# A decoder megakernel: its first layer reordered and written as a straight line

## The chip, the cores and the metric

One core of a Trainium2 chip runs the whole program in one launch. The metric is the device time of that core in microseconds, the median of several executions. The core's engines work from queues of their own, in order, and wait for each other through semaphores: TensorE (PE; its weight loads are PEld), VectorE (DVE), ScalarE (ACT), GpSimd (POOL) and SyncE (SP), which here only issues transfers.

## What is computed

Two decoder layers on x of 64 sequences x 128 tokens x 128 channels, all in float32, each sublayer followed by `x = layernorm(x + f(x))`: a linear attention with a cumulative sum, a cross attention of 16 heads, a mixture of experts, a selective scan, a second cross attention and a quantised feed-forward. The change touches only the first sublayer:

```python
def _L0_attn_ref(x, w_qkv, w_swiglu, w_out):
    qkv = jnp.einsum('btd,ed->bte', rms_norm(x), w_qkv)
    q, k, v = jnp.split(qkv, 3, axis=-1)
    q, k = rms_norm(q), rms_norm(k)
    w = jnp.exp(k)
    kv = jnp.cumsum(w * v, axis=1)
    w = jnp.cumsum(w, axis=1)
    y = jax.nn.sigmoid(q) * (kv / (w + 1e-06))
    u, g = jnp.split(jnp.einsum('bte,fe->btf', y, w_swiglu), 2, axis=-1)
    return x + jnp.einsum('btd,ed->bte', u * jax.nn.silu(g), w_out)

x = _layernorm(x + _L0_attn_ref(x, ...), axis=-1)
```

## The kernel before

`build` lays out memory, runs `setup`, and then six phases one after the other (a: `phase_aft`, b: first cross attention, m: experts, s: scan, c: second cross attention, q: feed-forward). x stays on the chip as [128 tokens, 64 sequences, 128]. Between phases stand full barriers: `open_signals` has SyncE raise every semaphore of the phase by one, `close_signals` has GpSimd clear them, and `finish_statistics` turns the batch-norm statistics that a phase left into mean and 1/deviation.

`setup` (L96, L102): SyncE asks for the four weights of phase a, ScalarE for the 45 others, one after the other; GpSimd sets constants. `phase_aft` first waits for the weights of a and s (ident is among the latter), then opens its block.

In `phase_aft` the 64 sequences go in 16 groups of GB = 4, so that a tile is 128 x 512. SyncE loads x group by group, each after the last has landed (L273), and then writes 33 fills of 1040 KB to DRAM for phase m (L278). Every other engine runs `in_group_steps`: three steps written out, a loop over g (1 to 13), three written out. A step works on several groups at once, by letters: a is group g+2, b g+1, c g, d g-1. The order within a step is fixed for each engine:

- TensorE: q, k and v of g+1 (`project`, L448, one signal after all twelve products), turning y of g (L468), turning x of g+2 (L439), g and u of g (`up`, L475, L478, one signal), sums of w and of w*v of g+1 (L458, L461, one signal), down product of g (L484).
- ScalarE: squares of x of g+2 (L316), squares of q and k of g+1 (L328, L331), copy of yT (L351), exp and tanh of g+1 (L339, L344), copy of xnT (L323), tanh of g (L356).
- GpSimd: 1/rms of x (L285, L288) and of q and k in one (L294, L298).
- VectorE: `mean_y` of g (add 1e-6 to den L391, reciprocal L394, gate L397, y L401), normalise x of g+2 (L380), `add_up` of g-1 (2x + o into `total` L415, statistics L167, copies into x and `core.stats` L169, L171), `weigh` of g+1 (w*v, L386), `hidden` of g (L407, L410).

All eight PSUM banks are in use, one tile each: turn, q, k, v, wsum, kvsum, u, g; the turned y goes into wsum's bank and the down product into u's. A signal's value in the loop is computed from g by register instructions.

Of the kernel before, what the change touches and what calls it, by code (L numbers as in the profile page):

```python
# [7 lines left out]
F32 = mybir.dt.float32  # L8
# [17 lines left out]
FILLS = 33  # L26
NO_ROW = 1e6
# [59 lines left out]
def setup(core):  # L87

    nc = core.nc
    with nc.Block() as block:  # L90
# [72 lines left out]
def leave(dve, nc, core, g, steps, total, stats):  # L163

    dve.wait_ge(steps.sem, steps.at(g, 1))
    for j in range(GB):
        last = nc.vector.bn_stats(stats[:, j, :], total[:, j, :])  # L167
    last.then_inc(steps.sem, 1)
    nc.vector.tensor_copy(core.x[:, ds(g * GB, GB), :], total[:, :, :])  # L169
    dve.wait_ge(steps.sem, steps.at(g, 2))  # L170
    nc.vector.tensor_copy(core.stats[:, ds(g * GB, GB), :], stats[:, :, :]).then_inc(steps.sem, 1)  # L171


def leave_one(dve, nc, core, i, steps, total, stats):

    dve.wait_ge(steps.sem, steps.at(i, 1))
    nc.vector.bn_stats(stats, total).then_inc(steps.sem, 1)
    nc.vector.tensor_copy(core.x[:, i, :], total)
    dve.wait_ge(steps.sem, steps.at(i, 2))
    nc.vector.tensor_copy(core.stats[:, i, :], stats).then_inc(steps.sem, 1)  # L180


def in_group_steps(eng, step):


    step(-2, "a")
    step(-1, "ab")
    step(0, "abc")
    with eng.Fori(1, NG - 2) as g:
        step(g, "abcd")  # L190
    step(NG - 2, "bcd")
    step(NG - 1, "cd")
    step(NG, "d")

def phase_aft(core):
    nc = core.nc  # L200
    x = core.x
    with ExitStack() as ctx:
# [14 lines left out]
        qk_ms = sb("a_qk_ms", [128, 2, GB])  # L217
        xn = sb("a_xn", [128, GB, 128])
        xnT = sb("a_xnT", [128, GT])
# [8 lines left out]
        total = sb("a_total", [128, GB, 128])  # L228
        stats = sb("a_stats", [128, GB, 6])
# [9 lines left out]
        o_ps = u_ps.rearrange("p (b d) -> p b d", b=GB)  # L239

        x_in = sig("a_x_in", 16)
# [6 lines left out]
        qkv_ready = sig("a_qkv_ready")  # L248
        qk_squared = sig("a_qk_squared")
        qk_eps = sig("a_qk_eps")  # L250
        qk_rms = sig("a_qk_rms")
# [30 lines left out]
        def _(pool):  # L282
# [19 lines left out]
            def step(g, stages):  # L302
                if "a" in stages:
                    x_rms_of(g + 2)
                if "b" in stages:
                    qk_rms_of(g + 1)
# [2859 lines left out]
```

## Time and profile before

| | us |
|---|---|
| median of 3 runs | 3586.96 (3586.45 to 3598.22) |
| profiled execution | 3601.83 |
| its span, first to last instruction | 3600.0 |
| of it: until the first square of x | 30.8 |
| first phase's last VectorE instruction ends | 258.9 |
| first instruction of the next phase on ScalarE | 266.6 |

Over the whole span TensorE is busy 77%, VectorE 70%, GpSimd 53%, ScalarE 47%; the granted TensorE clock was 0.892 of full on average. The first phase fills slices 1 to 3 of the page's forty (90 us each):

```profile
PE   4767887879878827777777777857999999998455
PEclk9988999978999958989889889998999999998555
DMA  5701000001144433333333333320000000000000
```

A digit is a share in tenths. TensorE is busy at 4, 7 and 6 tenths in the three slices, and DMA at 5, 7 and 0.

### The profile page before, as it was taken

What the parts mean: (1) busy time and instruction counts of PE and PEld (TensorE: products, weight loads), DVE (VectorE), ACT (ScalarE), POOL (GpSimd) and SP (SyncE); (2) the same over time, 40 slices, a digit from 0 to 9 for tenths busy, and PEclk for the clock granted to TensorE, in tenths of its full rate; (3) what the DMA queues carried; (4) which work ended last, traced back from release to release, by engine and by line L of the source; (5) the groups of instructions that cost most, each with busy time, mean ns of one, the idle gap of its engine ahead of it and who ended that gap; (6) DMA issues with size and microseconds to landing.
All of it is one profiled execution on the core that took longest, in us unless ns stands there. A gap on an engine that the chain in (4) does not pass through costs nothing. (4 is left out here: it accounts for less than half of the span.)

```text
span 3600.0 us, 53795 instructions
## 1 busy us (share of the span) xinstructions
PE 2787.7 (77%) x16569; PEld 1638.9 (46%) x16584; DVE 2503.4 (70%) x4015; ACT 1708.7 (47%) x3190; POOL 1897.4 (53%) x1698
## 2 busy tenths in 40 slices
PE   4767887879878827777777777857999999998455
PEld 3435555555645512323333333324666666666222
DVE  3768888845533335988988989994666666664787
ACT  3546666633222216555555555543444444443565
POOL 1216777745545546767767767762333333332444
PEclk9988999978999958989889889998999999998555
DMA  5701000001144433333333333320000000000000
GB/s 184 328 2 24 18 17 17 10 24 35 35 125 131 127 96 148 126 127 141 110 127 139 115 125 137 130 82 6 3 5 5 4 4 5 5 3 1 9 17 21
DMA packets 130113, 249.03 MB, mean 69 GB/s; under 512 B 41057, under 2 KB 97910, under 8 KB 109314
## 3 DMA queue, kind: packets, MB, share of 16 engines
q1 hardware_dynamic: 114480, 223.49, 18.1%
q0 software_dynamic: 9088, 16.94, 1.4%
q10 hardware_dynamic: 6354, 6.27, 0.6%
q8 instruction: 93, 1.52, 0.2%
q14 instruction: 98, 0.80, 0.1%
HBM read 189.34 MB, written 59.13 MB: 69 GB/s over the span
## 5 line engine op out<-in xcount | busy, mean ns | idle before, releaser
L1753 POOL TENSOR_TENSOR s_drive<-s_du,s_b_sb 128x1024 f32<-128x1024 f32 x256 | 602.1, 2355 | 288.0 <-DVE s_state_ps L1979 287.8
L1979 DVE TENSOR_TENSOR_SCAN s_state_ps<-s_decay_ps,s_drive 128x512 f32<-128x512 f32 x512 | 600.2, 1218 | 124.6 <-ACT s_decay_ps L1886 62.6
L2092 PE MATMUL s_y_ps<-s_read,w_ident 128*128 128x512 f32 x1024 | 540.6, 661 | 187.9 <-DVE s_read L1993 187.6
L1886 ACT ACTIVATE s_decay_ps<-s_delta,neg_rate 128x508 f32<-128x508 f32 x512 | 348.3, 686 | 388.9 <-DVE s_state_ps L1979 388.7
L2092 PEld LDWEIGHTS s_y_ps<-s_read,w_ident 128*128 128x128 f32 x1024 | 198.6, 207 | 512.3 <-DVE s_read L1993 298.7
L1993 DVE TENSOR_TENSOR s_read<-s_state_ps,s_c_sb 128x1024 f32<-128x1024 f32 x256 | 313.3, 1224 | 12.7 <-DVE s_state_ps L1979 1.4
L2315 ACT ACTIVATE c_pT<-c_turn_ps 77x512 f32<-77x512 f32 x256 | 148.7, 585 | 248.7 <-PE c_turn_ps L2516 248.6
L2249 POOL TENSOR_TENSOR x<-c_xs,w_c_bo 128x128 f32<-128x128 f32 x64 | 31.1, 486 | 427.4 <-DVE c_xs L2355 427.4
L1372 POOL DMA_INDIRECT m_y_scratch<-e_y,e_index x156 | 152.6, 978 | 135.6 <-DVE e_index L1406 56.5
L697 ACT ACTIVATE b_pT<-b_turn_ps 77x512 f32<-77x512 f32 x256 | 145.0, 590 | 117.8 <-PE b_turn_ps L822 117.8
L631 POOL TENSOR_TENSOR b_p<-b_p,b_top 128x1232 f32<-128x1232 f32 x64 | 143.9, 2248 | 93.9 <-DVE b_top L754 93.9
L2372 DVE TENSOR_TENSOR c_v<-c_f_ps,w_c_bv 77x512 f32<-77x512 f32 x128 | 87.9, 687 | 148.5 <-PE c_f_ps L2486 148.5
L2271 POOL TENSOR_TENSOR c_p<-c_p,c_norm 128x1232 f32<-128x1232 f32 x64 | 143.8, 2247 | 70.6 <-DVE c_norm L2395 70.6
L996 POOL DMA_INDIRECT m_rows_scratch<-m_xs,m_index x128 | 126.9, 991 | 100.3 <-DVE m_xs L1124 59.8
L2323 ACT ACTIVATE c_oT<-c_f_ps 128x512 f32<-128x512 f32 x128 | 76.4, 597 | 207.1 <-PE c_f_ps L2534 207.1
L2546 PE MATMUL c_turn_ps<-w_c_wo,c_oT 128*128 128x128 f32 x1024 | 136.2, 289 | 45.7 <-ACT c_pT L2315 44.9
L822 PE MATMUL b_turn_ps<-w_ident,b_p 128*77 128x128 f32 x1024 | 160.4, 291 | 14.3 <-POOL b_p L637 14.2
L2546 PEld LDWEIGHTS c_turn_ps<-w_c_wo,c_oT 128*128 128x128 f32 x1024 | 125.5, 200 | 73.5 <-issue 72.6
L637 POOL TENSOR_TENSOR b_p<-b_p,b_norm 128x1232 f32<-128x1232 f32 x64 | 143.9, 2248 | 22.0 <-DVE b_norm L760 21.9
L2516 PEld LDWEIGHTS c_turn_ps<-w_ident,c_p 128*77 128x77 f32 x1024 | 123.5, 148 | 69.3 <-issue 47.6
L2516 PE MATMUL c_turn_ps<-w_ident,c_p 128*77 128x128 f32 x1024 | 153.9, 278 | 1.0 <-ACT c_pT L2315 1.0
L2377 DVE TENSOR_REDUCE c_top<-c_s_ps 128x16 f32<-128x1232 f32 x64 | 92.3, 1441 | 81.7 <-PE c_s_ps L2500 81.7
(366 smaller groups left out, 6535.8 us busy)
## 6 DMA issues: line engine op xcount, KB each, us to landing
s_b_sb<-s_bc_scratch SPq DMA_DIRECT2D x64, 1024.0 KB, 4.6
s_c_sb<-s_bc_scratch SPq DMA_DIRECT2D x64, 1024.0 KB, 4.7
m_rows_scratch<-fill SPq DMA_DIRECT2D x33, 1040.0 KB, 26.2
e_w<-in_m_we_dram SPq DMA_DIRECT2D x39, 384.0 KB
e_xg<-m_rows_scratch SPq DMA_DIRECT2D x39, 260.0 KB
k_y<-m_y_scratch SPq DMA_DIRECT2D x32, 256.0 KB, 3.8
x<-in_x_dram SPq DMA_DIRECT2D x16, 256.0 KB, 2.8
out_dram<-q_result SPq DMA_DIRECT2D x16, 256.0 KB, 2.3
```

The lines of the kernel that those rows point to most:

```text
L631: nc.gpsimd.tensor_tensor(p[:, s, :, :], p[:, s, :, :], top[:, s, :].unsqueeze(2).broadcast_to([128, heads, S2]), ALU.subtract).then_inc(l ...
L697: nc.scalar.activation(pT[:, j, :, :], turn_ps[0:S2, j % 2, :].rearrange("p (r t) -> p r t", t=128), ACT.Copy).then_inc(pT_ready.sem, 1)
L822: last = nc.tensor.transpose(turn_ps[0:S2, j % 2, r * 128:(r + 1) * 128], p[:, s, per * r + j, :], core.ident[:, :])
L1372: nc.gpsimd.indirect_dma_start(y_dram[:, :], bass.IndirectOffsetOnAxis(index[:, t % y_slots, j:j + 1], 0), y[:, t % y_slots, j, :], None, ...
L1753: nc.gpsimd.tensor_tensor(drive[:, n % 2, :, :], du[:, s, :, :], b_sb[:, n, :].unsqueeze(1).broadcast_to([128, halves, GT]), ALU.mult).the ...
L1886: nc.scalar.activation(decay[:, m, :, 1:], delta[:, s, m, :].rearrange("p (b t) -> p b t", t=T)[:, :, 1:], ACT.Exp, scale=core.neg_rate[:, ...
L1979: nc.vector.tensor_tensor_scan(state[:, h, :], decay[:, h, :, :].rearrange("p b t -> p (b t)"), drive[:, n % 2, h, :], 0.0, ALU.mult, ALU. ...
L1993: nc.vector.tensor_tensor(read[:, n % deep, :, :], state[:, :, :], c_sb[:, n // per_chunk % 2, n % per_chunk, :].unsqueeze(1).broadcast_to ...
L2092: last = nc.tensor.matmul(y_ps[:, m, :], core.ident[:, :], read[:, n % deep, m, :], start=False, stop=(n == states - 1))
L2315: nc.scalar.activation(pT[:, per * r:per * (r + 1), :], turn_ps[0:S2, r % 2, :].rearrange("p (j t) -> p j t", t=128), ACT.Copy).then_inc(p ...
L2516: last = nc.tensor.transpose(turn_ps[0:S2, r % 2, j * 128:(j + 1) * 128], p[:, i % 2, per * r + j, :], core.ident[:, :])
L2546: last = nc.tensor.matmul(y_ps, oT[:, b, :], core.w["c_wo"][:, b, :], start=(b == 0), stop=(b == blocks - 1))
```

## The change

- `setup`: ScalarE asks for the first three groups of x and no weight; SyncE asks for the weights of phase a, ident now first among them. The other weights follow on SyncE in the phase, after the loads of the other 13 groups of x and before the fills.
- No wait ahead of the phase's block; TensorE alone waits for its weights.
- No loops: `over_periods` writes out 21 steps from g = -4 to 16 for all engines. Stages are further apart: squares and normalisation of x at g+4, turning x at g+3, projections at g+2, sums and y at g+1, up at g, down and the addition at g-1.
- q, k and v have signals of their own, k first; so have the squares of q and k, the two sums, and g and u. xnT has two buffers.
- Normalising x moves from VectorE (four instructions) to GpSimd (one on 128x512). GpSimd's 1/rms of q and k is split in two. Adding 1e-6 to den moves from VectorE to ScalarE (Identity with a bias).
- The turned y uses the turn bank; the down product uses v's bank, so that v of g+2 waits for the addition of g-1.
- The addition writes x in place, and the statistics go straight to `core.stats`; `total`, `stats` and both copies go.
- ident stays in memory to the end.

```diff
 def setup(core):
         @block.scalar
         def _(act):
-            for phase in "sbmcq":
-                for name in WEIGHTS[phase]:
-                    act.dma_start(core.w[name][:], core.ins[name]).then_inc(core.landed[phase].sem, 16)
+            for g in range(EARLY):
+                act.dma_start(core.x[:, g * GB:(g + 1) * GB, :],
+                              core.ins["x"][g * GB:(g + 1) * GB, :, :].rearrange("b t d -> t b d")
+                              ).then_inc(core.x_early[g].sem, 16)
...
-        o_ps = u_ps.rearrange("p (b d) -> p b d", b=GB)
+        o_ps = v_ps
...
+        def over_periods(step):
+            for g in range(-4, NG + 1):
+                step(g)
-        open_signals(nc, signals, [core.landed["a"], core.landed["s"]])
+        open_signals(nc, signals, [])
...
         def _(sp):
-            with sp.Fori(0, NG) as g:
-                sp.wait_ge(x_in.sem, x_in.at(g, 0))
+            for g in range(EARLY, NG):
+                if g > EARLY:
+                    sp.wait_ge(x_in.sem, x_in.at(g - EARLY, 0))
...
+            for phase in "bmscq":
+                for name in WEIGHTS[phase]:
+                    sp.dma_start(core.w[name][:], core.ins[name]).then_inc(core.landed[phase].sem, 16)
             for n in range(FILLS):
...
         def _(pool):
+            def normalise(g):
+                pool.wait_ge(x_rms.sem, x_rms.at(g, 1))
+                if g >= 1:
+                    pool.wait_ge(x_turned.sem, x_turned.at(g - 1, 1))
+                nc.gpsimd.tensor_tensor(xn[:, :, :], x[:, g * GB:(g + 1) * GB, :],
+                                        x_ms[:, :].unsqueeze(2).broadcast_to([128, GB, 128]),
+                                        ALU.mult).then_inc(x_normed.sem, 1)
+            def step(g):
+                if on(g + 4):
+                    x_rms_of(g + 4)
+                    normalise(g + 4)
+                if on(g + 2):
+                    k_rms_of(g + 2)
+                    q_rms_of(g + 2)
...
         def _(act):
+            def raise_den(g):
+                act.wait_ge(wsum_ready.sem, wsum_ready.at(g, 1))
+                if g >= 1:
+                    act.wait_ge(y_steps.sem, y_steps.at(g - 1, 2))
...
+                nc.scalar.activation(den[:, :], wsum_ps[:, :], ACT.Identity,
+                                     bias=den_eps[:, 0:1]).then_inc(den_ready.sem, 1)
+            def step(g):
+                if on(g):
+                    copy_yT(g)
+                if on(g + 1):
+                    raise_den(g + 1)
+                if on(g + 4):
+                    square_x(g + 4)
+                if on(g + 3):
+                    copy_xnT(g + 3)
+                if on(g + 2):
+                    square_k(g + 2)
+                    square_q(g + 2)
+                    exp_k(g + 2)
+                if on(g):
                     tanh_g(g)
+                if on(g + 2):
+                    tanh_q(g + 2)
...
         def _(dve):
             def weigh(g):
                 dve.wait_ge(w_ready.sem, w_ready.at(g, 1))
+                dve.wait_ge(v_ready.sem, v_ready.at(g, 1))
+                if g >= 1:
+                    dve.wait_ge(kvsum_ready.sem, kvsum_ready.at(g - 1, 1))
...
             def add_up(g):
+                here = x[:, g * GB:(g + 1) * GB, :]
                 dve.wait_ge(o_ready.sem, o_ready.at(g, 1))
+                nc.vector.scalar_tensor_tensor(here, here, 2.0, o_ps[:, :, :], ALU.mult,
+                                               ALU.add).then_inc(added.sem, 1)
+                dve.wait_ge(added.sem, added.at(g, 1))
+                for j in range(GB):
+                    nc.vector.bn_stats(core.stats[:, g * GB + j, :], x[:, g * GB + j, :])
+            def step(g):
+                if on(g + 1):
+                    weigh(g + 1)
+                if on(g - 1):
+                    hidden(g - 1)
+                if on(g + 1):
+                    mean_y(g + 1)
+                if on(g - 1):
+                    add_up(g - 1)
...
         def _(pe):
+            def project_v(g):
+                if g >= 1:
+                    pe.wait_ge(kv_ready.sem, kv_ready.at(g - 1, 1))
+                if g >= 3:
+                    pe.wait_ge(added.sem, added.at(g - 3, 1))
+                project(g, v_ps, 2, v_ready)
+            def step(g):
+                if on(g):
                     turn_y(g)
+                if on(g + 1):
+                    sum_w(g + 1)
+                if on(g + 3):
+                    turn_x(g + 3)
+                if on(g + 1):
+                    sum_kv(g + 1)
+                if on(g + 2):
+                    project_k(g + 2)
+                    project_q(g + 2)
+                if on(g - 1):
+                    down(g - 1)
+                if on(g):
                     up(g)
+                if on(g + 2):
+                    project_v(g + 2)
+            pe.wait_ge(core.landed["a"].sem, core.landed["a"].value)
+            over_periods(step)
```

## Rows read from the trace of the kernel before

**Rows 1.** Eight periods: us; busy us PE, PEld, DVE, ACT, POOL; clock; DMA share; GB/s.

```profile
102.35:204.73 102.38, 75.33 (x386) 48.07 (x385) 80.42 (x144) 56.69 (x280) 24.92 (x33) 0.97 0.57 237
```

**Rows 2.** One period on VectorE; timeline: start, us, engine, line, operation [idle before].

```profile
102.35 3.35 DVE L394 RECIPROCAL a_den<-a_den 128x512 f32<-128x512 f32 x1
...
107.16 0.86 DVE L380 TENSOR_SCALAR a_xn<-x,a_x_ms 128x128 f32 x4
107.94 0.68 DVE L415 SCALAR_TENSOR_TENSOR a_total<-x,a_u_ps 128x512 f32<-128x512 f32 x1
...
109.44 0.41 DVE L169 COPY x<-a_total 128x512 f32 x1
...
113.10 0.69 DVE L407 SCALAR_TENSOR_TENSOR a_th_g<-a_th_g,a_g_ps 128x512 f32<-128x512 f32 x1 [1.31 <-ACT a_th_g L356]
...
114.43 0.68 DVE L391 TENSOR_SCALAR a_den<-a_wsum_ps 128x512 f32<-128x512 f32 x1
```

**Rows 3.** TensorE in the same period.

```profile
101.77 1.16 PE L484 MATMUL a_u_ps<-w_a_woutT,a_h 128*128 128x128 f32 x8 [1.29 <-DVE a_h L410]
...
104.55 1.06 PE L448 MATMUL a_v_ps<-w_a_wqkvT,a_xnT 128*128 128x128 f32 x8
107.30 0.66 PE L468 MATMUL a_wsum_ps<-w_ident,a_y 128*128 128x128 f32 x4 [1.69 <-DVE a_y L401]
...
111.32 1.10 PE L458 MATMUL a_wsum_ps<-a_w_kv,w_upper 128*128 128x512 f32 x2 [0.54 <-ACT a_w_kv L339]
```

**Rows 4.** ScalarE and GpSimd in the same period.

```profile
101.78 1.01 POOL L288 TENSOR_TENSOR a_x_ms<-a_x_ms,minus_half 128x4 f32<-128x4 f32 x1
...
105.65 0.28 ACT L328 ACTIVATE a_square<-a_q_ps 128x128 f32<-128x128 f32 x1 [4.22 <-PE a_v_ps L448]
...
108.17 1.72 POOL L298 TENSOR_TENSOR a_qk_ms<-a_qk_ms,minus_half 128x8 f32<-128x8 f32 x1
...
109.93 1.14 ACT L339 ACTIVATE a_w_kv<-a_k_ps,a_qk_ms 128x128 f32<-128x128 f32 x4 [1.26 <-POOL a_qk_ms L298]
...
112.42 0.66 ACT L356 ACTIVATE a_th_g<-a_g_ps 128x512 f32<-128x512 f32 x1
```

**Rows 5.** The opening: last weight request, table load, first square.

```profile
22.33 0.46 ACTq L102 DMA_DIRECT2D w_q_wd<-in_q_wd_dram  x1
24.88 1.28 ACT L316 ACT_TABLE_LOAD   x1 [24.88 <-PEq L54]
...
30.79 0.31 ACT L316 ACTIVATE a_square<-x 128x128 f32<-128x128 f32 x1 [4.63 <-DMA x<-in_x_dram]
```

**Rows 6.** TensorE's first projection of q.

```profile
36.20 2.07 PE L448 MATMUL a_q_ps<-w_a_wqkvT,a_xnT 128*128 128x128 f32 x8 [0.69 <-ACT a_xnT L323]
```

**Rows 7.** VectorE: first and last reciprocal, last instruction of the phase.

```profile
51.66 3.35 DVE L394 RECIPROCAL a_den<-a_den 128x512 f32<-128x512 f32 x1
...
243.06 3.35 DVE L394 RECIPROCAL a_den<-a_den 128x512 f32<-128x512 f32 x1
...
258.73 0.17 DVE L171 COPY stats<-a_stats 128x24 f32<-128x24 f32 x1
```

**Rows 8.** GpSimd by line, whole span: 128x512 multiplication and addition; busy, mean ns.

```profile
L1512 POOL TENSOR_TENSOR k_y<-k_y 128x512 f32<-128x512 f32 x16 | 22.2, 1391 | 24.0 <-DMA k_y<-m_y_scratch 23.9
...
L2711 POOL TENSOR_TENSOR q_xs<-q_xs,rstd 128x512 f32<-128x512 f32 x16 | 16.9, 1058 | 3.5 <-POOL q_xs L2707 3.2
```

**Rows 9.** ScalarE in the next phase: Exp (L691), then Identity (L672).

```profile
281.60 1.23 ACT L691 ACTIVATE b_p<-b_p 128x1232 f32<-128x1232 f32 x1 [0.95 <-POOL b_p L631]
282.74 0.48 ACT L672 ACTIVATE b_xs<-x,b_shift,rstd 128x128 f32<-128x128 f32 x1
```

**Rows 10.** SyncE's requests: start, us until the last one is issued, count.

```profile
25.18 49.87 SPq L273 DMA_DIRECT2D x<-in_x_dram  x16
75.26 62.87 SPq L278 DMA_DIRECT2D m_rows_scratch<-fill  x33
```

**Rows 11.** From issue to landing, the 33 fills (L278).

```profile
DMA to landing us min/median/max: 4.9/26.2/30.2
```

More of the change, by code:

```diff
@@ L160, in _ @@
                                            ALU.add, ALU.mult).then_inc(folded, 1)
[L163 to L193, printed above, removed]
 def phase_aft(core):
@@ L302, in step @@
[L302 to L306, printed above, removed]
-            in_group_steps(pool, step)
+            def normalise(g):
[5 more added lines that the diff above has]
+                                        ALU.mult).then_inc(x_normed.sem, 1)
@@ L335, in exp_tanh, with square_k @@
[L335 to L337 removed]
+                if g >= 2:
+                    act.wait_ge(v_ready.sem, v_ready.at(g - 2, 1))
+                nc.scalar.activation(xnT[:, g % 2, :], turn_ps[:, :], ACT.Copy).then_inc(xnT_ready.sem, 1)
+            def square_k(g):
+                act.wait_ge(k_ready.sem, k_ready.at(g, 1))
+                for j in range(GB):
+                    last = nc.scalar.activation(square[:, 1, j, :], k_ps[:, j, :], ACT.Square,
+                                                scale=D ** -0.5, accum_out=k_ms[:, j:j + 1])
+                last.then_inc(k_squared.sem, 1)
@@ L440, in turn_x @@
                 last.then_inc(x_turned.sem, 1)
-            def project(g):
-                pe.wait_ge(xnT_ready.sem, xnT_ready.at(g, 1))
-                pe.wait_ge(th_q_ready.sem, th_q_ready.at(g, 0))
-                pe.wait_ge(kv_ready.sem, kv_ready.at(g, 0))
-                for which, bank in enumerate((q_ps, k_ps, v_ps)):
-                    for j in range(GB):
-                        last = nc.tensor.matmul(bank[:, j, :], xnT[:, j * 128:(j + 1) * 128],
-                                                core.w["a_wqkvT"][:, which * 128:(which + 1) * 128],
-                                                start=True, stop=True)
-                last.then_inc(qkv_ready.sem, 1)
@@ L453, in sum_up, with project, project_k @@
-            def sum_up(g):
+            def project(g, bank, which, done):
+                for j in range(GB):
+                    last = nc.tensor.matmul(bank[:, j, :], xnT[:, g % 2, j * 128:(j + 1) * 128],
+                                            core.w["a_wqkvT"][:, which * 128:(which + 1) * 128],
+                                            start=True, stop=True)
+                last.then_inc(done.sem, 1)
+            def project_k(g):
+                pe.wait_ge(xnT_ready.sem, xnT_ready.at(g, 1))
+                if g >= 1:
+                    pe.wait_ge(w_ready.sem, w_ready.at(g - 1, 1))
+                project(g, k_ps, 1, k_ready)
```

240 lines of the change are left out of this document (117 added, 123 removed).

## The prediction

> **What bounds the kernel now.** I read the engines' busy time by stretch first, then one period of the first phase on each engine, then its opening and its end. The change touches only that phase: it holds 259 of 3600 us, so what can be won or lost lies there. In its steady part sixteen groups of four sequences pass at one every 102.38 / 8 = 12.80 us, with VectorE busy 80.42 / 8 = 10.05 us of them, ScalarE 7.1, GpSimd 3.1 [rows 1]. No engine is full. The period is a ring of waits, and the starts show it: the last product of v ends at 104.55 + 1.06 = 105.61, and the squares of q, queued on ScalarE, start at 105.65 [rows 3, 4]. GpSimd's power on 8 columns runs 108.17 to 109.89, Exp starts at 109.93, tanh of g ends at 113.08 [rows 4], VectorE goes on with th_g at 113.10 after 1.31 us of idling [rows 2], h follows, and then TensorE runs down, q, k and v in one row, as at 101.77 to 105.61 [rows 3], because all three projections stand behind the down product and ScalarE waits for v before it squares q. That is, from start to start, 2.52 (squares and GpSimd's addition) + 1.76 (power) + 3.17 (exp to tanh of g) + 1.47 (th_g and h) + 3.88 (down to v) = 12.8 us. The other thing the rows show is the opening: ScalarE asks for the last weight at 22.33, the phase's block opens at 24.88, and the first square starts at 30.79 when x has landed [rows 5]. Thirty microseconds hold no arithmetic.
>
> **The ring after the change.** It falls apart: k has its own signal, squares need q and k alone, q and k stand ahead of down, and a group's stages are spread over six periods. I looked for the rings that are left, with time zero at the end of v for group g+2.
>
> Ring A goes through VectorE and both ends of TensorE's step, since v reuses the bank of the down product: v waits for add_up(g-1), which VectorE does after the reciprocal. From zero: turning y 0.66, sum of w 1.10 [rows 3], overlapping a little, so 1.6; the new ScalarE copy with bias, costed like tanh of g with the same 128x512 from PSUM, 0.66 [rows 4], so den is there at 2.3. From the reciprocal's start to the addition's start the rows show 107.94 - 102.35 = 5.59, of which the normalisation between them (107.94 - 107.16 = 0.78) goes away: 4.81, so the addition starts at 7.1 and ends 0.68 later [rows 2], and v takes 1.06 [rows 3]. With four hand-overs of 0.04 (105.61 to 105.65) this is 9.0 us. weigh, th_g and h fit before 2.3: three instructions of 0.69. The statistics, now written straight to their place, lie beside v.
>
> Ring B goes through ScalarE and GpSimd: the squares of x (four, half of q and k's eight, 1.1 to 1.3), GpSimd's addition and power (0.27 + 1.01, rows at 101.78) [rows 4], the normalisation moved there, addition and power for k (1.3), then exp, tanh of g, tanh of q and the copy of yT (the same four kinds as 109.93 to 113.08, 3.15) and the new copy (0.5 to 0.66). The normalisation has no row in this phase. The nearest is a 128x512 multiplication with a factor per row, 1.06 us; another on 128x512 took 1.39 [rows 8]. By the first the ring is 8.7, by the second 9.0 us. I take 1.06, the same shape and operation, so it just doesn't bind.
>
> The engines alone: VectorE loses the normalisation 0.86, the addition to den 0.68, both copies 0.41 and 0.17 [rows 2, 7], so 10.05 - 2.12 = 7.9 and some gaps, 8.3. ScalarE gains 0.66: 7.8. GpSimd goes to about 5.0, since one power on 8 columns (1.72) becomes two on 4 (1.01 each) plus the normalisation; nobody but ring B waits for it. TensorE does the same work: 3.84 for down, q, k, v, four products of 1.10, two turns of 0.66 [rows 3], 9.6 if nothing overlapped, about 8.4 as neighbours do overlap (the four took 0.96 each). So the period is **9.0**, with ends 8.4 (engines alone) and 9.6 (TensorE without overlap).
>
> **Opening.** ScalarE now asks for three pieces of x, SyncE for five weights. At 0.46 each [rows 5] the latter end at 3.05. From there I copy the old distance 22.79 to 24.88, 2.09 us, and the table load of 1.28 [rows 5]. Nine more signals are raised one by one; that costs between nothing and 2.09 x 9 / 23 = 0.8, I take 0.4. x, asked for in the first microsecond, took 5.6 us from 25.18 to 30.79 [rows 5, 10] and so is there by 6.4. The first square starts at 6.9: 23.9 us gained. From the square to the first reciprocal the old kernel takes 51.66 - 30.79 = 20.9 [rows 5, 7]. The new order puts turning x of group 1 ahead of k of group 0, so this is squares 1.3, power 1.3, normalisation 1.1, all three again for group 1 (3.6), turn 1.1, k and q at the low clock 1.8 each (2.07 with the tail [rows 6]), squares and exp 1.1 each, sum of w 2.0, copy 0.7: 16.9, with hand-overs 17.3. The first reciprocal starts at 24.2.
>
> **The waits added** are mostly splits of old ones. v's wait for add_up holds the step's last product and, behind it, the turning of the next y; that is ring A. The turning of y waits for the next copy of xnT, done a period earlier. The requests for 44 weights move from ScalarE to SyncE, behind 13 loads of x (one per 49.87 / 15 = 3.3 us) and ahead of the fills [rows 10]: 5.4 + 13 x 3.3 + 44 x 0.46 puts the first fill at about 69 instead of 75, and their last request at 132. They land some 26 us later [rows 11], at 158, before this phase ends; were it to end before 150, the next phase's loads would queue behind them. The x of group 3 is asked for at 5.4 and used at 24, so loads stay hidden. Identity on ScalarE could have called for another table; in the next phase it follows Exp directly, 281.60 + 1.23 to 282.74 [rows 9], so it costs nothing. Constant waits instead of computed ones I cost at nothing: in the old period they lie beside other engines' work.
>
> **End and sum.** From the last reciprocal to the phase's last instruction: 258.90 - 243.06 = 15.8 [rows 7]. After: hidden(14) and down(14) now stand ahead of the last up product (+2), tanh of g no longer waits for u and the copies are gone (-2). I take 16.0, from 14.9 to 16.9. Intervals between reciprocals: the first 9.6 at the low clock, fourteen of 9.0. Last instruction: 24.2 + 9.6 + 126.0 + 16.0 = 175.8 instead of 258.9, 83.1 less; nine more semaphores to clear, 0.4, and rounding leave **82**. The profiled execution took 3601.83 (span 3600.0); it becomes 3520. The median of the runs is 15 us lower, 3586.96, so the forecast is **3505**. The rest of the kernel is unchanged.
>
> **What speaks against it in the notes.** In the old period a copy of 128x512 on VectorE (109.44 to 109.85, 0.41 us) ran inside GpSimd's power (108.17 to 109.89) without being held up [rows 2, 4]. The Trainium skill (SBUF — State Buffer, "SBUF: two separate sides") says that these two engines share a port pair as an exclusive lock, when VectorE's operation has two SBUF inputs or a two-port mode. By that rule the copy should have stood until 109.89; on 8 columns the trace doesn't agree. It doesn't show a GpSimd operation on 512 columns beside the gate, the one VectorE instruction of this phase with two large SBUF inputs.
>
> **Rivals.** (1) GpSimd's normalisation and the gate block each other, or ring B turns out longer than its rows. Ring A then grows by up to one normalisation, 1.06 [rows 8]: period 10.1, 16 us more, **3521**. For it: by ring A the gate comes 5.8 us after v, just where the normalisation ends. Against: the copy above. Chance 0.17. The Trainium skill's port rule, named above, would give this outcome.
> (2) Only part of the ring dissolves, the change doesn't do what it says: the period stays near 12 because some wait still ties two steps. Then opening and ramp give 27.5 and the periods 12: 27.5 + 15 x 0.8 = 39.5 less, **3547**. Chance 0.09, of it 0.02 for a ring that keeps its whole length and an opening that gains less.
> (3) The period falls to the engines' own 8.4: 9 us less, **3496**. Chance 0.10.
> (4) Slower: TensorE's clock. It had 0.97 of full over the eight periods [rows 1] and was low at the start, where q took 2.07 instead of 1.06 [rows 6, 3]. If the new order left it at the low level, its 8.4 us become 8.4 x 1.95 = 16.4 and it is the bound: 15 x 3.6 - 27.5 = 26 more, **3613**. It decides against the change from a period of 12.8 + 27.5 / 15 = 14.6. Against it: TensorE would be busier than now, idle only half a microsecond before v. Chance 0.03.
> (5) Slower: the loops are now straight code, fetched during the fills, when DMA is full. If four fetches stood on the ring for 26.2 us each [rows 11], that is 105 us: **3610**; more than three decide. Chance 0.02.
> The forecast itself has 0.59.
>
> **Range and chances.** The five ways and the forecast's own ends (period 8.7 to 9.6, opening and end 3 us, and the spread of 12 us that the three runs before show) give 3490 to 3535. A measurement here tells 0.5% from no change, so faster means below 3569: the forecast, (1), (3) and most of (2), 0.93. Same 0.02, slower 0.05.
>
> **What would show it.** The first square at 7, the first reciprocal at 24, reciprocals 9.0 apart, v waiting for the addition and the addition 4.8 after the reciprocal's start, TensorE's clock above 0.9 in the phase, the phase's last VectorE instruction at 176, and the next phase as long as before. Wrong would be: gate or reciprocal longer than 0.69 and 3.35, Exp waiting on GpSimd for over 1.5 us, idle time put down to nothing on several engines at once while fills run, or a time lost after 185 us.

## The result, and the profile after

The kernel after takes 3487.81 us in the median (3484.19 to 3497.28), the kernel before 3591.65 (3586.45 to 3598.22) in the executions taken for the comparison: a ratio of 0.9716 (0.9699 to 0.9733). The profiled execution took 3497.28 us where the old one took 3601.83, so 104.5 us of its span went, and 82 were forecast. The ends of five phases can be read off one instruction that each of them ends with, the square root in `finish_statistics`. Start of that instruction in the kernel before, and then in the kernel after:

```profile
L134 ACT ACTIVATE a_root<-rstd x1: 256/256/256, 262.8 to 262.8; 128x64 f32<-128x64 f32 x1
L134 ACT ACTIVATE b_root<-rstd x1: 256/256/256, 731.6 to 731.6; 128x64 f32<-128x64 f32 x1
L134 ACT ACTIVATE m_root<-rstd x1: 256/256/256, 1333.5 to 1333.5; 128x64 f32<-128x64 f32 x1
L134 ACT ACTIVATE s_root<-rstd x1: 256/256/256, 2440.4 to 2440.4; 128x64 f32<-128x64 f32 x1
L134 ACT ACTIVATE c_root<-rstd x1: 256/256/256, 3338.9 to 3338.9; 128x64 f32<-128x64 f32 x1
```

```profile
L136 ACT ACTIVATE a_root<-rstd x1: 256/256/256, 180.9 to 180.9; 128x64 f32<-128x64 f32 x1
L136 ACT ACTIVATE b_root<-rstd x1: 256/256/256, 657.1 to 657.1; 128x64 f32<-128x64 f32 x1
L136 ACT ACTIVATE m_root<-rstd x1: 257/257/257, 1252.6 to 1252.6; 128x64 f32<-128x64 f32 x1
L136 ACT ACTIVATE s_root<-rstd x1: 256/256/256, 2335.6 to 2335.6; 128x64 f32<-128x64 f32 x1
L136 ACT ACTIVATE c_root<-rstd x1: 257/257/257, 3234.0 to 3234.0; 128x64 f32<-128x64 f32 x1
```

Differences of these starts, and of the spans' ends (3600.0 and 3495.5), are the lengths of the phases, in us:

| phase | before | after | difference |
|---|---|---|---|
| a, the changed one | 262.8 | 180.9 | -81.9 |
| b, cross attention | 468.8 | 476.2 | +7.4 |
| m, experts | 601.9 | 595.5 | -6.4 |
| s, scan | 1106.9 | 1083.0 | -23.9 |
| c, second cross attention | 898.5 | 898.4 | -0.1 |
| q, feed-forward | 261.1 | 261.5 | +0.4 |

So the changed phase gained what was forecast, and the scan, which no line of the change touches, gained 24 us. Eight periods of the first phase in the kernel after (columns as in [rows 1]):

```profile
60.81:133.61 72.80, 66.48 (x387) 46.06 (x386) 65.46 (x89) 60.42 (x290) 40.34 (x56) 1.00 1.01 418
```

The period is 72.80 / 8 = 9.10 us in place of 12.80. TensorE is busy 91% of it, VectorE 90%, ScalarE 83%, GpSimd 55%; TensorE's clock stood at its upper level throughout. The opening, on ScalarE, against [rows 5]:

```profile
0.74 1.58 ACTq L102 DMA_DIRECT2D x<-in_x_dram  x3
5.57 1.28 ACT L324 ACT_TABLE_LOAD   x1 [5.57 <-PEq L55]
6.86 0.31 ACT L324 ACTIVATE a_square<-x 128x128 f32<-128x128 f32 x1
```

The first square starts straight behind the table load. The first reciprocal, on VectorE:

```profile
23.41 3.35 DVE L421 RECIPROCAL a_den<-a_den 128x512 f32<-128x512 f32 x1 [1.40 <-ACT a_den L374]
```

One period, engines interleaved in order of time, to be read beside [rows 2 to 4]:

```profile
60.59 0.39 ACT L324 ACTIVATE a_square<-x 128x128 f32<-128x128 f32 x1
...
60.81 3.35 DVE L421 RECIPROCAL a_den<-a_den 128x512 f32<-128x512 f32 x1 [0.25 <-ACT a_den L374]
...
62.01 0.20 POOL L272 TENSOR_TENSOR a_x_ms<-a_x_ms,rms_eps 128x4 f32<-128x4 f32 x1 [3.74 <-ACT a_square L324]
62.29 1.01 POOL L275 TENSOR_TENSOR a_x_ms<-a_x_ms,minus_half 128x4 f32<-128x4 f32 x1
...
63.38 1.04 POOL L282 TENSOR_TENSOR a_xn<-x,a_x_ms 128x512 f32<-128x512 f32 x1
...
64.27 0.70 DVE L424 SCALAR_TENSOR_TENSOR a_gate<-a_th_q,a_den 128x512 f32<-128x512 f32 x1
...
64.37 0.65 POOL L288 TENSOR_TENSOR a_k_ms<-a_k_ms,rms_eps 128x4 f32<-128x4 f32 x1
...
65.10 1.01 POOL L291 TENSOR_TENSOR a_k_ms<-a_k_ms,minus_half 128x4 f32<-128x4 f32 x1
...
65.61 0.68 DVE L447 SCALAR_TENSOR_TENSOR x<-x,a_v_ps 128x512 f32<-128x512 f32 x1
66.08 0.20 POOL L297 TENSOR_TENSOR a_q_ms<-a_q_ms,rms_eps 128x4 f32<-128x4 f32 x1
66.14 1.14 ACT L355 ACTIVATE a_w_kv<-a_k_ps,a_k_ms 128x128 f32<-128x128 f32 x4 [1.21 <-POOL a_k_ms L291]
...
66.43 1.13 PE L479 MATMUL a_v_ps<-w_a_wqkvT,a_xnT 128*128 128x128 f32 x8 [0.21 <-DVE x L447]
...
69.69 0.39 ACT L324 ACTIVATE a_square<-x 128x128 f32<-128x128 f32 x1
```

ScalarE waits 1.21 us for GpSimd's power of k, which stands behind the normalisation (63.38). It is ring B of the prediction that closes here, from one set of squares of x to the next: squares to GpSimd's first addition 62.01 - 60.59 = 1.42, addition and power 1.37, normalisation 0.99, addition for k 0.73, power to Exp 66.14 - 65.10 = 1.04, and from Exp to the next squares 69.69 - 66.14 = 3.55; together 9.10. The addition for k takes 0.65 us beside the gate. The same form took 0.20 for x at 62.01 and for q at 66.08, and so did the additions in the kernel before. The normalisation just ahead of it (63.38 to 64.42) overlaps the gate's start by 0.15 us, and neither of the two is longer than elsewhere.

And the waits of VectorE in the scan phase, before and then after (us in all, times, longest):

```profile
DVE s_state_ps L1979 <- ACT s_decay_ps L1886: 62.6, 15, 43.8
DVE s_state_ps L1979 <- issue: 28.5, 5, 5.8
DVE s_state_ps L1979 <- DVE s_read L1993: 27.9, 147, 0.2
```

```profile
DVE s_state_ps L2029 <- ACT s_decay_ps L1936: 65.9, 17, 46.8
DVE s_state_ps L2029 <- DVE s_read L2043: 27.6, 145, 0.2
```

Five times the scan instruction stood still for some 5.7 us, for nothing that the profile shows as a releaser, once at each wrap of the scan's loop (six turns, so five wraps). The kernel after has none of it. What the transfers show around one of these stalls (1572.1 to 1577.92), in the kernel before from 1571 to 1579, is that code was fetched there, and that a load of 1 MB landed between two of its packets:

```profile
DMA  0000100000006996994994995210000000000100
q1 hardware_dynamic: 144, 1.05, 31.8%
q14 instruction: 3, 0.02, 1.0%
s_c_sb<-s_bc_scratch SPq DMA_DIRECT2D x1, 1024.0 KB, 4.7
```

The first 1 is a packet of code (q14) at 1572.0, the high digits that follow are the load, and the other packets of code come at 1576.1, near the load's end, and at 1578.5, behind the stall. q14 moves code in packets of 8 KB, VectorE's among it, since its packets over the whole kernel rise from 98 to 99 and 101 with the longer fillings of VectorE's code below, while q8's stay at 93. q8 moves code in packets of 16 KB; that this is TensorE's is likely, and no run tested it. Over the scan phase q14 has 38 packets in the kernel before and 12 in the kernel after.

### The profile page after: what moved, and what is told of

The parts are those of the page before. It is cut to its first block and busy times, and to the rows that moved or that the text cites. A ratio compares the mean times of both kernels' runs of the same rounds, so it can differ in the third digit from the quotient of the medians.

```text
span 3495.5 us, 53312 instructions
## 1 busy us (share of the span) xinstructions
PE 2774.1 (79%) x16584; PEld 1631.1 (47%) x16584; DVE 2472.3 (71%) x3903; ACT 1718.9 (49%) x3206; POOL 1928.1 (55%) x1747
```

## The experiments on the first phase

Six kernels ask which part of the change gives the 82 us and which ring sets 9.10. Phase lengths below are read from their own traces in the way shown above, and ratios are to the kernel before on the same chip.

**The opening alone**: the kernel before with the new opening and its old loops.

```diff
-            for phase in "sbmcq":
-                for name in WEIGHTS[phase]:
-                    act.dma_start(core.w[name][:], core.ins[name]).then_inc(core.landed[phase].sem, 16)
+            for g in range(EARLY):
+                act.dma_start(core.x[:, g * GB:(g + 1) * GB, :], ...).then_inc(core.x_early[g].sem, 16)
...
+            for phase in "bmscq":
+                for name in WEIGHTS[phase]:
+                    sp.dma_start(core.w[name][:], core.ins[name]).then_inc(core.landed[phase].sem, 16)
```

> The kernel before with the opening alone changed: three groups of x asked for by ScalarE in the setup, the other weights on SyncE behind the loads of x, no wait ahead of the block, ident first and kept in memory. Loops and orders as before. My account: first square at 6.9 us, period 12.8 as before, first phase's last VectorE instruction at 259 - 24 = 235, whole 3563. ident's place in memory changes here as in the kernel after, VectorE's code does not move: theory P has the scan phase at 1107 us, rival M at 1083 and the whole at 3539.

It took 3565.1 us (0.9923 of the kernel before, 0.9894 to 0.9952). The first phase is 238.1 us, 24.7 shorter; the scan is 1103.3 us, with 38 fetches and `L1989 <- issue: 28.8, 5, 5.9`, as before. So the opening gives its own 24.7 us, and neither it nor the place of ident in memory takes the scan's stall away.

**The straight line alone**: `for g in range(1, NG - 2)` in place of the `Fori` of `in_group_steps` in the kernel before.

> The kernel before with the loop over the groups written out in the first phase and nothing else changed. My account: the period stays 12.80 us and the first phase ends at 259, since waits on constants instead of computed ones lie beside work. Rival: the loop's register instructions cost something in each period, 12.5 or less. Written out, VectorE's code moves the scan's loop from 1178 to 1375, so by what the shifts showed the scan phase is likely to take 1078 us instead of 1107: the whole 3565, all of it from a phase that the edit doesn't touch.

The first phase took 260.2 us with a period of 12.78: writing the loop out is worth some 3 us there, none of it in the period. The scan took 1087.1 us with 37 fetches and five short stalls. That was not expected, and it is taken up below.

**k bound to v again**: the kernel after, with the squares of k held back until v is there.

```diff
             def square_k(g):
-                act.wait_ge(k_ready.sem, k_ready.at(g, 1))
+                act.wait_ge(v_ready.sem, v_ready.at(g, 1))
```

> The kernel after, but ScalarE squares k only when v is ready, as before the change. v waits for the addition, the squares for v, Exp and both tanh for them, the copy of yT and of den stand behind these on ScalarE, and the reciprocal behind den. Ring theory: squares 2.2, GpSimd 1.3, exp and tanhs 2.5, copies 1.2, reciprocal to addition 4.8, addition and v 1.8: a period of about 13.9 us, longer than the old kernel's 12.8, first phase longer by 5 x 15 = 72 us. Rival (signals of their own are a detail, the wider spacing of the stages gave the gain): below 10.

3569.12 us; the first phase is 260.5 us, as long as before the change, opening included. From the fourth reciprocal on, periods ran from 14.17 to 15.83, over the 13.9 expected. ScalarE in it:

```profile
133.26 0.28 ACT L337 ACTIVATE a_square<-a_k_ps 128x128 f32<-128x128 f32 x1 [6.47 <-PE a_v_ps L479]
```

```profile
0.00:260.50 260.50, 173.54 (x768) 120.39 (x768) 133.37 (x183) 125.11 (x579) 76.56 (x125) 0.83 0.47 178
```

The second fence is the whole phase by engine, columns as in [rows 1]. One wait puts 6.47 us of idle time back into ScalarE's period and undoes 80 us. The short period thus needs k's own signal. Whether that signal alone would be enough, in the old order and spacing of the stages, no run shows: v stands last in the new step and waits for the addition, so binding k to it may cost more here than the same binding did there. The granted clock over the phase is 0.83, where the kernel after has 0.95; the matmuls at the lower level are a likely part of the excess over 13.9, which no run separated.

**The down product first**: the kernel after, with `down(g - 1)` ahead of k and q on TensorE.

```diff
-                if on(g + 2):
-                    project_k(g + 2)
-                    project_q(g + 2)
                 if on(g - 1):
                     down(g - 1)
+                if on(g + 2):
+                    project_k(g + 2)
+                    project_q(g + 2)
```

> The kernel after with the down product ahead of k and q in TensorE's step again. Ring theory: k is ready 0.9 us later, its squares end at about the time at which GpSimd is done with the normalisation anyway (64.4 in the period from 61 us), so Exp comes 0.3 to 0.5 us later and the period grows from 9.1 to 9.4 to 9.6; 5 to 7 us in all. Rival (the order of projections and down product is what broke the old ring): the period goes to 11 or more.

A period of 9.15, where 9.4 to 9.6 were expected, and 181.1 us for the phase. The order that gives the change part of its name is worth 0.05 us a period. GpSimd's addition for k takes 0.20 us here, as it starts later, in the last 0.08 us of the gate (64.23, having waited 0.45 us for the squares of k), so nearly all that the order saves on one side the held-up addition takes back on the other.

**The normalisation last on GpSimd**: the kernel after, with 1/rms of k and q ahead of it.

```diff
                     x_rms_of(g + 4)
-                    normalise(g + 4)
                 if on(g + 2):
                     k_rms_of(g + 2)
                     q_rms_of(g + 2)
+                if on(g + 4):
+                    normalise(g + 4)
```

> The kernel after with GpSimd's normalisation of x moved behind the 1/rms of k and q in each step. In the kernel after the period is 9.10 us; GpSimd's small addition for k starts beside the gate on VectorE and takes 0.65 us instead of 0.20, and Exp waits for it. Ring theory: with k's 1/rms ahead of the normalisation this ring is about 1 us shorter, the ring over the addition and v binds at 8.8 us, twelve periods save 0.3 each, the whole 3 to 5 us less. Rival (the period is bound by VectorE and TensorE alone): it stays 9.1. Port theory: a small GpSimd operation is stretched only where it meets the gate; if none meets it, all take 0.20.

3480.63 us, 0.9685 of the kernel before (0.9649 to 0.9722): the lowest ratio of the kernels that were timed several times, though its interval overlaps that of the kernel after. The first phase is 174.4 us, 6.5 less than the kernel after, and the period 8.80: about 4 us come from the periods and 2.5 from the first two intervals, 7.75 and 8.25 instead of 9.36 and 9.10. GpSimd in one period:

```profile
67.01 0.20 POOL L272 TENSOR_TENSOR a_x_ms<-a_x_ms,rms_eps 128x4 f32<-128x4 f32 x1 [3.67 <-ACT a_square L325]
67.29 1.01 POOL L275 TENSOR_TENSOR a_x_ms<-a_x_ms,minus_half 128x4 f32<-128x4 f32 x1
68.60 0.20 POOL L288 TENSOR_TENSOR a_k_ms<-a_k_ms,rms_eps 128x4 f32<-128x4 f32 x1 [0.30 <-ACT a_square L338]
68.88 1.01 POOL L291 TENSOR_TENSOR a_k_ms<-a_k_ms,minus_half 128x4 f32<-128x4 f32 x1
69.85 0.20 POOL L297 TENSOR_TENSOR a_q_ms<-a_q_ms,rms_eps 128x4 f32<-128x4 f32 x1
70.13 1.01 POOL L300 TENSOR_TENSOR a_q_ms<-a_q_ms,minus_half 128x4 f32<-128x4 f32 x1
71.10 1.04 POOL L282 TENSOR_TENSOR a_xn<-x,a_x_ms 128x512 f32<-128x512 f32 x1
```

All sixteen additions for k are back at 0.20 (mean 199 ns; 537 in the kernel after), as the gate at 69.26 now lies beside a power. Ring B has lost both the normalisation and the stretched addition, and what is left at 8.80 is VectorE, busy 65.04 of 70.40 us over eight periods, with one idle stretch of 0.46 a period.

**The normalisation back on VectorE**: the kernel after, with `normalise` as four instructions on VectorE, ahead of the addition, and none on GpSimd.

> The kernel after with the normalisation of x back on VectorE (four instructions of 128x128 ahead of the addition, as in the kernel before). Ring theory: it stands on the ring over the addition and v, so the period grows by its 0.78 us from that ring's 8.8, to 9.6. GpSimd's additions all take 0.20. Rival (moving it to GpSimd brought nothing, since GpSimd's ring binds anyway): 9.1 or less. VectorE's code grows, the scan's loop starts at 1327 (place 47 of 256), where theory P expects no gaps.

Period 9.58, first phase 184.5 us, 3493.88 us in one execution. Moving it to GpSimd is worth 0.5 us a period, and a further 0.3 if it stands last there. Of the phase it gives only 3.6 us, because the first interval here is 7.58 us and in the kernel after 9.36. In this kernel GpSimd has no normalisation, and one of its additions for q is held up all the same:

```profile
110.98 0.69 DVE L424 SCALAR_TENSOR_TENSOR a_gate<-a_th_q,a_den 128x512 f32<-128x512 f32 x1 [0.46 <-DVE a_den L421]
111.22 0.51 POOL L289 TENSOR_TENSOR a_q_ms<-a_q_ms,rms_eps 128x4 f32<-128x4 f32 x1
```

It ends at 111.73, 0.06 us behind the gate's end. The one for k in the kernel after starts at 64.37 and ends at 65.02, 0.05 behind the gate's end at 64.97. So what holds them up is the gate and not the normalisation, and an addition that starts inside the gate isn't over before it.

## The experiments on the scan

The scan's body is a loop of 295 instructions on VectorE, as the trace's records count one turn. (I had counted 232, which is what is left without 63 waits on semaphores.) The change makes VectorE's code ahead of it longer. The theory: the stall depends on where the loop lies in the code. The rivals: the new place of weights in memory (answered by the opening alone, above), and something that the change does for good. The edit is always the same, instructions on VectorE that do nothing for the result:

```diff
+            for n in range(PAD):
+                nc.vector.memset(pad[:, n:n + 1], 0.0)
```

> The kernel before with 84 one-column memsets on VectorE in the setup block, where VectorE waits for ScalarE's weight requests anyway; the first layer is untouched. With the block's branch they move all later VectorE code on by 86 instructions, nearly to where it lies in the kernel after. Theory P (the scan phase's loop on VectorE, 232 instructions, lies over three 8 KB code pages before and over two after, and a turn of it then costs a fetch): the five idle gaps of 5.5 to 5.8 us before L1979 vanish, the scan phase takes 1083 us instead of 1107, the whole 3563 instead of 3587, the first phase ends at 259 as before. Rival M (the scan gains because ident lies elsewhere in memory or because its weights came earlier): gaps and 1107 us stay, 3587. Rival C (chance, another state of the clock): the scan changes by less than 5 us either way.

84 of them in the kernel before: 3562.46 us, 0.9898 (0.9862 to 0.9934). The scan takes 1078.9 us instead of 1106.9, with 14 fetches and no stall:

```profile
DVE s_state_ps L1987 <- ACT s_decay_ps L1894: 62.3, 16, 46.7
DVE s_state_ps L1987 <- DVE s_read L2001: 27.8, 146, 0.2
```

Eighty-four useless instructions make the kernel before one per cent faster. Then 20 of them:

> The same with 20 memsets, a shift of 22 instructions, which leaves the loop on three pages. Theory P: the five gaps of 5.5 us stay and the scan phase takes 1107 us. If memsets in the setup as such changed the scan, it would be shorter here too.

3563.93 us, scan 1077.9, 13 fetches, no stall. My count of where the pages lie was wrong; that the place matters was not. Two kernels asked for the length of the pattern. They were to move the loop by exactly 128 and 256 instructions; by the records of the traces they moved it by 126 and 254, and the two fillings above by 20 and 84:

> The kernel before with 126 memsets on VectorE in the setup, which move its later code on by exactly 128 instructions, 8 KB, one code page as it is fetched here. Shifts of 22 and 86 took the five gaps in the scan away. If the place within an 8 KB page decides, they come back here: scan phase 1107 us. If the place within 16 KB decides, or the absolute place, they stay away: 1078.

> The same with 254 memsets, a shift of exactly 256 instructions, 16 KB. If the place within 8 or 16 KB decides, the gaps come back: 1107 us. If they stay away with both shifts, no period of 16 KB exists, and what makes the old place a bad one stays open.

Both have 38 fetches again, and scans of 1100.2 and 1097.0 us. In the first:

```profile
DVE s_state_ps L1987 <- issue: 12.6, 5, 2.6
DVE s_state_ps L1987 <- POOL s_drive L1761: 10.1, 5, 2.2
```

There are two stalls a wrap here, 3.6 us apart, of some 2.0 and 2.5 us, one put down to GpSimd only because it happened to end last: 22.7 us in all. So stalls come at shifts of 0, 126 and 254 and not at 20 and 84, a pattern that fits a length of 128 instructions, if such a length fills one packet of 8 KB.

Then the kernel after, at the fillings where I thought the stall would return:

> The kernel after with 43 one-column memsets on VectorE at the start of the first phase, where VectorE idles until 21 us. They bring the scan's loop back to the place within a code page that it has in the kernel before (26 of 128 by my count). Theory P: five gaps of 5.5 us come back, the scan phase takes 1107 us, the whole 24 us more than the kernel after, about 3512; the first phase is as in the kernel after, last VectorE instruction at 177. Rivals M and C: scan phase 1083, whole 3488.

> The kernel after with 147 one-column memsets on VectorE at the start of the first phase, hidden in its idle 21 us. The first round showed that my count of pages was wrong: a loop that starts at instruction 1178 of VectorE's code stalls, at 1200, 1263, 1264 and 1306 it doesn't, so what counts is the place within 256 instructions (154 stalls; 176, 239, 240 and 26 don't). 147 memsets bring the loop to 1410, place 154 again. Theory P: five gaps of 5.5 us come back, scan phase about 1104, the whole 24 us above the kernel after, 3512. Rival: the stall belongs to the old kernel's order of code in some other way, scan phase 1080, whole 3488.

It did not: 3486.55 us (0.9689; 0.9656 to 0.9723) and 3496.96 us (0.972; 0.9687 to 0.9753), scans of 1078.1 and 1081.4, 12 fetches in each. The places had been worked out from the count of 232 and were not the ones meant. That left open whether the kernel after was merely lucky. Three more places, on one chip:

> The kernel after with 64 instructions of filling on VectorE ahead of the work, so that the scan's loop starts 66 instructions later in VectorE's code. If the stall at the loop's wrap (5 turns by 2.5 to 5.8 us, 37 or 38 code fetches in the scan in place of 12 to 14) is a matter of where the loop lies in pages of 128 instructions, one or two of the three shifts 66, 87 and 108 show it here, since shifts of 0, 45 and 149 did not: the scan then takes some 1100 us and has about 38 fetches. If the kernel after is rid of it for good, each of the three shows 12 to 14 fetches and a scan of 1078 to 1083 us.

> As after_pad64, with the loop 87 instructions later. By the place in pages of 128: scan near 1100 us with about 38 fetches in one or two of the three; by the other theory 12 to 14 fetches and 1078 to 1083 us.

> As after_pad64, with the loop 108 instructions later. By the place in pages of 128: scan near 1100 us with about 38 fetches in one or two of the three; by the other theory 12 to 14 fetches and 1078 to 1083 us.

| filling | time of one execution | scan | fetches in it |
|---|---|---|---|
| 64 | 3408.26 | 1079.0 | 13 |
| 85 | 3424.14 | 1088.0 | 38 |
| 106 | 3414.72 | 1088.7 | 37 |

The stall is back at 85 and 106. So the kernel after isn't rid of it; it has a good place. Last, two of them timed several times:

> The kernel after with 85 instructions of filling on VectorE, the place at which the stall was seen again. If the gain beyond the forecast was the stall's absence, its scan takes 24 us more than after_pad64_timed's where a wrap costs 5.7 us (9 us where it costs 2.5 us), and its time over the kernel before has a ratio near 0.978 to 0.980 (3505 + 2 for the filling, over 3592), against 0.971 for after_pad64_timed. By the other theory, that the 24 us are the change's own, both have the same ratio within 0.002.

> The kernel after with 64 instructions of filling, a place without the stall: scan 1078 to 1083 us, 12 to 14 fetches, ratio to the kernel before near 0.971 (0.973 at most). By the other theory the same as after_pad85_timed.

85: 3502.47 us, 0.974 (0.9714 to 0.9766), scan 1088.2, 38 fetches. 64: 3484.87 us, 0.9697 (0.9674 to 0.9719), scan 1081.1, 13 fetches. The direction is as expected, the size isn't: the scans differ by 7.1 us, not 24 (the medians by 17.6, with intervals that still touch; the other phases of the two profiles differ by 6 us more without any such reason). VectorE in the scan of the first:

```profile
DVE s_state_ps L2034 <- POOL s_drive L1808: 9.7, 5, 2.0
```

One stall of 2 us a wrap. There is a short and a long form, then. Around a short one, from 1750 to 1755 in the same kernel (the stall ends at 1753.38):

```profile
DMA  0000000000200000000959999979799797999946
q1 hardware_dynamic: 134, 1.04, 50.6%
q14 instruction: 1, 0.01, 0.6%
s_c_sb<-s_bc_scratch SPq DMA_DIRECT2D x1, 1024.0 KB, 4.3
```

The packet of code is the 2 at 1751.3, a microsecond ahead of the 1 MB load. The stall ends 2.1 us behind it. In the long form a second packet is waited for: in all five long stalls of the kernel before, and in the five of the opening alone, the first packet comes 5.5 to 6.0 us ahead of the stall's end and the second 1.8 us ahead of it, with the load between the two. In the straight-line kernel, too, the form is the short one, five stalls of 1.9 to 2.2 us, and its scan lies 8 to 9 us over the good ones.

The records of VectorE around the branch that closes a turn show why one place differs from another. Without a stall the next instruction comes 0.3 us after the branch, with one 2.8 to 3.1 us after it. The kernel before then has a second gap, of 3.4 to 3.9 us, two instructions further on, and the kernels with 126 and 254 fillings one of 2.2 to 2.6 us four instructions further on. Counted along VectorE's code, with earlier loops once, these second gaps lie at instructions 1471, 1599 and 1727, which are 128 apart. If packets end there, all nineteen traces fit one rule:

| the loop starts so many instructions into a packet | kernels | packets that it touches | at each wrap |
|---|---|---|---|
| 6, 25, 49, 70 | after and its edits that leave VectorE's code as long; after with 147, 43, 64 | 3 | no stall |
| 18, 82, 85 | before with 20, 84; normalisation on VectorE | 3 | no stall |
| 91, 112, 118 | after with 85, 106; straight line | 4 | one stall of 1.9 to 2.2 us |
| 124 | before with 126, 254 | 4 | two stalls of 1.9 to 2.7 us |
| 126 | before, opening alone | 4 | one stall of 5.4 to 5.9 us |

A loop of 295 touches four packets of 128 when it starts more than 89 into one. The long form is a loop that starts two instructions before the end of a packet, so that two packets are waited for in a row. That the 1 MB load makes the second one late is likely, as it comes 3.7 to 4.2 us after the first, where packets with no load between them come 2.0 to 2.7 us apart; no run without the load tested it. Nor did a filling put the kernel after at 124 or 126, so its long form was not brought back: of the 24 us of the scan, 7 to 10 were.

## Why the prediction was right in its phase and wrong in its range

| step of the prediction | predicted | measured |
|---|---|---|
| first square of x | 6.9 | 6.86 |
| first reciprocal | 24.2 | 23.41 |
| first interval between reciprocals | 9.6 | 9.36 |
| period | 9.0 | 9.10 |
| last reciprocal to last instruction | 16.0 | 16.5 |
| last VectorE instruction ends | 175.8 | 176.8 |
| gain of the first phase | 82 | 81.9 |
| rest of the kernel | 0 | -22.6 |

**The step that failed** is the last sentence of the sum, "The rest of the kernel is unchanged". It is true of the program text and was taken to be true of the time. The forecast of 3505 and the range down to 3490 both stand on it; the measured 3487.81 lies 2 us below the range. (With 3591.65, the old kernel's median in the comparison, in place of 3586.96 the same sum gives 3510.) The rest of the kernel took 22.6 us less, of which the scan gives 23.9 (the other phases together lost 1.3): five stalls of 5.7 us (28.5 in the waits of VectorE) that the kernel before has, and that the new length of VectorE's code takes away, since it moves the loop's start from 126 to 6 in a packet. The row stood in the trace of before and I hadn't asked for it, since the change does not touch that phase. Rival (5) thought of code fetches, but only of those of the new straight line, in the first phase and as a loss. No such loss shows: the phase came out at its forecast.

Seen without the stall on either side, the sum roughly holds: on one chip the filled kernel before took 3562.46 us and the filled kernel after 3486.55, 75.9 apart. The first phases of the two profiles are 262.8 - 179.2 = 83.6 us apart; the other phases took 9.8 of that back, none of it by a stall.

**The opening** is right in its parts: the block opened at 5.57 instead of 5.5, and x had landed by then. The opening alone gives 24.7 us.

**The ring** was the right one to look for, but it is ring B that closes and not ring A. The prediction had ring B at 8.7 with a normalisation of 1.06; it took 1.04. What it didn't have is 0.45 us of the addition for k held up beside the gate: 8.7 + 0.45 is the 9.10, within the rounding. That is a part of rival (1), which had named this pair of engines and allowed for a whole normalisation. It was another instruction, and it cost less than half. That the period came so near its 9.0 is in part luck: ring A was priced at least 0.2 too long, and ring B missed a term of 0.45. The Trainium skill (SBUF — State Buffer, "SBUF: two separate sides") has the two engines share a port pair as an exclusive lock when VectorE reads two SBUF inputs and GpSimd reads SBUF. On this pair the traces agree: 0.65 beside the gate, 0.20 with the gate elsewhere, in the same program but for the order, and a held-up addition ends 0.05 to 0.07 behind the gate. On another pair they do not: with the normalisation last, the gate (69.26, 0.69 us) starts inside a power of GpSimd (68.88, 1.01 us) and neither is longer than elsewhere.

Ring A, 9.0 by the prediction, was somewhat too long: with ring B out of the way the period is 8.80, so it can't be more than that.

**Rival (2)**, a ring that stays near 12, is what the kernel with k bound to v shows, even worse at 14.8. **Rival (3)**, the engines' own 8.4, isn't reached: with the normalisation last VectorE is busy 8.13 us of 8.80, with one idle stretch of 0.46. **Rival (4)**: the clock didn't fall in the kernel after (0.95 over the phase), but it did in the one with the long waits (0.83), so the fear belonged to a kernel that idles.

**Waits and requests**: v waits 0.21 us for the addition, as forecast; the fills begin at 61.44 instead of 69, since a load of x took 34.05 / 13 = 2.6 us instead of 3.3, and nothing hung on it. Identity on ScalarE called for no table: the only load of the phase's work is the one at 5.57.

**Left open**: phase b took 476.2 us and its old length is 468.8; over all kernels run it lay between 467.1 and 476.9 without any order that an edit explains. Phase m lay between 588.7 and 601.9 in the kernels run on most chips, phase c between 887.9 and 901.9. None has a cause that a run showed. How much of the fall from 12.80 to 9.10 belongs to the signals, the order and the spacing of the stages was not taken apart either.

## What to carry to other kernels

Before you write that the rest is unchanged, ask for the idle time put down to "issue" at the wrap of every later loop: code that grows or shrinks ahead of a loop moves it, and here that decided 7 to 28 us on a loop of 295 instructions and five wraps. An experiment with a few useless instructions ahead of the loop costs little and tells a gain of the edit from a gain of the place.

In a ring over several engines, first split the signal that couples the late product to the early one (80 us here, in the new order); then look at the order on the engine with least work, since on GpSimd it gave 0.3 us a period more, and the reordering of products on TensorE 0.05.

## What the runs showed of the hardware

- VectorE's code comes in packets of 8 KB. A loop of 295 instructions was fetched anew at each wrap where it touched four stretches of 128 instructions, and not where it touched three: 37 or 38 fetches in the scan, or 12 to 14. The Trainium skill (Runtime: NRT & Kernel Launch, "Instruction fetch mechanics") says that a taken branch to a page outside the two that are held stalls until the page is fetched. That there is such a stall, the traces agree: 2.8 to 3.1 us from the branch to the next instruction instead of 0.3. The same section gives blocks of 16 KiB, 256 instructions; for this engine the packets of 8 KB and the gaps at 1471, 1599 and 1727 speak for 128.
- One such stall cost 1.9 to 2.7 us, or 5.4 to 5.9 where two packets were waited for in a row, with a load of 1 MB between them.
- A GpSimd addition of four columns that started inside a VectorE instruction with two SBUF inputs of 512 columns and was held up ended 0.05 to 0.07 us behind it, and took up to 0.70 us instead of 0.20. Powers and a multiplication of GpSimd that overlapped the same instruction were not longer.
- Chips differ, mostly in one phase: on two of them the experts took 518 to 521 us in every kernel, on the others 589 to 602, and the kernel before took 3505 to 3507 us instead of 3592 to 3597.
